# TensorE's sums of units 2 and 4 behind two u projections, and two step sizes and one scan input later on GpSimd

## The reference

```python
x = x + relu(sum over k of Xk @ Wk[k] + bk[k])       # graph layer, Xk = transition^k @ layernorm(x)
x = x + fc2(mamba(fc1(layernorm(x))))
# mamba: u, z = split(W_in h); u = silu(causal conv of 4 taps(u) + conv_b)
# dt, B, C = split(W_xproj u); delta = softplus(W_dt dt + b_dt); A = -exp(A_log)
h = exp(d_t[..., None] * A) * h + (d_t * u_t)[..., None] * B_t[:, None, :]   # scan over t
y_t = einsum('bds,bs->bd', h, C_t)
# y = (y + u * D) * silu(z), then W_out
```

## Time and profile before

| | us |
|---|---|
| median of 3 runs (3755.41 to 3759.54) | 3758.61 |
| the profiled execution's own time | 3757.91 |
| its span | 3756.1 |

### The profile page before, as it was taken

The page is one execution under the profiler, slowest core; times in us unless marked ns, Lnnn a source line. Parts: engine busy times, 40 slices in busy tenths (PEclk is TensorE's granted clock), DMA queues, the critical chain, the costliest instruction groups (busy, mean ns, idle before and its releaser), DMA issues.

```text
span 3756.1 us, 43683 instructions
## 1 busy us (share of the span) xinstructions
PE 3466.2 (92%) x11130; PEld 1957.4 (52%) x11130; DVE 3524.5 (94%) x2877; ACT 2954.1 (79%) x6578; POOL 3415.5 (91%) x1703
## 2 busy tenths in 40 slices
PE   6899999999999999999999999999999999999888
PEld 3555555555555555555555555555555555555434
DVE  0499999999999999999999999999999999999998
ACT  2588878888878888888788888788887888887774
POOL 0299999999999999999999999999999999999998
PEclk8899999999999999999999999999999999999999
DMA  3111101111100111110111110111110111110110
GB/s 111 53 56 58 58 10 52 55 58 58 58 23 38 55 58 58 58 39 22 58 55 58 58 56 8 55 55 58 58 58 9 53 55 58 58 54 12 42 51 9
DMA packets 50720, 183.68 MB, mean 49 GB/s; under 512 B 7356, under 2 KB 33220, under 8 KB 42086
## 3 DMA queue, kind: packets, MB, share of 16 engines
q1 hardware_dynamic: 48898, 174.17, 12.0%
q10 hardware_dynamic: 1636, 7.83, 0.5%
HBM read 164.15 MB, written 17.83 MB: 48 GB/s over the span
## 4 chain that ended last, share of the span: by engine, by line
POOL 54%; issue 31%; PE 7%; DVE 3%; ACT 3%; POOLq 1%; DMA 0%; SPq 0%; ACTq 0%; DVEq 0%
POOL st L425 40%; POOL st L416 7%; POOL delta L398 3%; POOL du_sb L406 3%; PE y_ps L771 2%; DVE st L953 1%; DVE st L965 1%; PE d_ps L808 1%; ACT dec L491 1%; POOL rstd L383 1%; POOLq L192 1%; PE g L924 1%; ACT L491 0%; PE dec L700 0%; DMA rows<-bk_dram 0%
## 5 line engine op out<-in xcount | busy, mean ns | idle before, releaser
L425 POOL TENSOR_TENSOR st<-st,bc 128x1024 f32<-128x1024 f32 x1024 | 2407.4, 2365 | 173.6 <-DVE st L965 172.8
L965 DVE TENSOR_TENSOR_SCAN st<-dec,st 128x1024 f32<-128x1024 f32 x1024 | 2313.0, 2274 | 12.1 <-POOL st L416 6.0
L771 PE MATMUL y_ps<-st,ident 128*128 128x512 f32 x4096 | 1947.4, 609 | 179.3 <-POOL st L425 177.6
L491 ACT ACTIVATE dec<-delta,decay 128x254 f32<-128x254 f32 x4096 | 1688.5, 462 | 286.4 <-DVE st L965 284.5
L771 PEld LDWEIGHTS y_ps<-st,ident 128*128 128x128 f32 x4096 | 748.1, 191 | 998.2 <-issue 628.0
L953 DVE TENSOR_TENSOR st<-du,bc 128x1024 f32<-128x1024 f32 x736 | 883.3, 1200 | 2.5 <-ACT du L477 2.2
L416 POOL TENSOR_TENSOR st<-du_sb,bc 128x1024 f32<-128x1024 f32 x288 | 681.5, 2367 | 0.1
L539 ACT ACTIVATE u<-d_ps,bconv,chan 128x256 f32<-128x256 f32 x256 | 130.0, 558 | 335.7 <-PE d_ps L808 335.7
L990 DVE SCALAR_TENSOR_TENSOR u<-d_ps,chan,u 128x250 f32<-128x250 f32 (+2 forms) x768 | 307.5, 468 | 58.7 <-ACT u L539 58.5
L808 PE MATMUL d_ps<-xnT,wxz 128*128 128x256 f32 x1024 | 257.0, 396 | 7.8 <-DVE u L990 7.1
L828 PE MATMUL d_ps<-xnT,wxz 128*128 128x256 f32 x1024 | 246.5, 384 | 14.6 <-ACT zs L552 14.2
(11 more groups left out here) (111 smaller groups left out, 2509.0 us busy)
## 6 DMA issues: line engine op xcount, KB each, us to landing
bc<-bc_dram SPq DMA_DIRECT2D x64, 2048.0 KB, 9.8
xg<-x_dram SPq DMA_DIRECT2D x32, 256.0 KB, 11.4
x_dram<-xg SPq DMA_DIRECT2D x32, 256.0 KB, 2.0
last_x<-x_dram SPq DMA_DIRECT2D x32, 256.0 KB, 2.6
out_dram<-last_x SPq DMA_DIRECT2D x32, 256.0 KB, 2.1
bc<-w_inT_dram ACTq DMA_DIRECT2D x1, 4096.0 KB, 13.9
adjt<-adjT_dram SPq DMA_DIRECT2D x32, 128.0 KB, 11.1
bc<-w_out_dram ACTq DMA_DIRECT2D x1, 2048.0 KB
```

The costliest lines, as they stand in the source:

```text
L425: nc.gpsimd.tensor_tensor(st[:, sl, :, :, :], st[:, sl, :, :, :], bc[:, p, 1, SU * q:SU * q + SU, None, :].to_broadcast([P, SU, 2, T]), AL ...
L491: a = nc.scalar.activation(dec[:, v % 2, s, j, :].rearrange("p (b t) -> p b t", b=PAIR)[:, :, 1:], delta[:, p, 2 * i + j, :].rearrange("p ...
L771: mm = nc.tensor.matmul(y_all, ident[:, :], st[:, sl, s, :, :].rearrange("p j t -> p (j t)"), start=False, stop=(q == Q - 1 and s == SU - ...
L965: nc.vector.tensor_tensor_scan(h, dec[:, v % 2, :, :, :].rearrange("p s j t -> p (s j t)"), h, 0.0, ALU.mult, ALU.add).then_inc(S["scanned ...
```

## The change

The sum of unit 2 moves from step 3 to step 4, where it stands behind the u projection and ahead of sum 3. The sum of unit 4 moves from step 5 to step 6, behind the u projection and ahead of sum 5. The step size of channel pair 2 moves from step 2 to step 10, that of pair 3 from step 6 to step 14, and the scan input of pair 2 from step 9 to step 11, each behind the product of its step.

```diff
-POOL_DELTAS = {0: 1, 2: 2, 6: 3}
-POOL_DUS = {2: 1, 9: 2, 17: 3}
+POOL_DELTAS = {0: 1, 10: 2, 14: 3}
+POOL_DUS = {2: 1, 11: 2, 17: 3}
@@ body of the TensorE list, in `if scan:`
                         if v % Q == 2:
                             state_sum(pe, k, p, v - 2)
-                        if v % Q != 1 and v > 0:
+                        if v in (4, 6):
+                            state_sum(pe, k, p, v - 2)
+                        if v % Q != 1 and v > 0 and v not in (3, 5):
                             state_sum(pe, k, p, v - 1)
```

## The result

The changed kernel takes 3736.4 us (median of 6 runs, 3729.5 to 3742.2) against 3757.1 (median of 6, 3755.4 to 3759.5) for the kernel before: ratio 0.9943, 95% interval 0.9933 to 0.9953. It is faster by some 21 us. I had forecast 3710 with a range of 3698 to 3728, so the gain is 21 us in place of the 48 that I worked out. Its runs also differ more among each other (13 us) than those before (4 us).

What follows compares the result with a forecast made beforehand. VectorE, 94% busy, was taken as the bound, GpSimd as a second. 28 bodies going from 111.93 to 110.4 us give 42.8, with the first and last bodies 48.4 us: 3710 us, range 3698 to 3728.

Steps and rivals of the forecast that it cites:

- The tap waits go: VectorE's convolution taps at steps 5 and 7: waits for ScalarE's u projection copy fall from 58.5 to 0 to 10 us.
- The gate, paced by product 6, becomes the limit: VectorE's gate at step 10 waits about 0.25 us for sum 7, behind GpSimd's product 6; a body takes 110.36 us.
- Body 1, body 30, body 31: Gains beside the 28 bodies: 2.7 us up to body 1's taps, 2.0 in body 30 less 0.3, 1.2 in body 31.
- Half clock behind the remaining gap: TensorE, behind about 2.0 us idle ahead of the first projection: costs some 1.6 us, 0.05 on the mean body.
- What I listed behind the projection: TensorE from step 4: projection, graph, sum 2, sum 3, graph, projection, sum 4, sum 5, all within 14.8 us.
- Rival 3: Half clock on TensorE's gapless stretch behind sum 6, 1.6 us each time on gate and scan 16: 3772 us; chance 5%.
- Rival 2: GpSimd's lateness felt at the second gate, step 18: 3739 us, or 3724 for half; chance 16% with the half.
- The rule weighed: Idle gaps between TensorE's bursts throttle it: the shorter first gap helps, the wait for product 6 could slow the gate.

Runs made afterwards that it cites:

- old-pool kernel: Changed kernel with sum 2 directly behind the projection of step 4, but GpSimd's step sizes and scan input where they were before the change: 3752.9 us, ratio 0.9987.
- inject kernel: Changed kernel with sum 2 directly behind the projection of step 4, and GpSimd's inject of unit 8 at step 6 behind product 6: 3698.6 us, ratio 0.9844.
- sums_only: Changed kernel with the new order of the sums, but GpSimd's step sizes and scan input where they were before: 3756.5 us, ratio 0.9997.
- pool_only: Kernel before the change, with only GpSimd's step sizes and scan input moved later as in the changed kernel: 3746.9 us, ratio 0.9973.
- sum2_first: Changed kernel with sum 2 directly behind the projection of step 4, ahead of the graph layer's first block: 3710.8 us, ratio 0.9878.
- block2_early: Changed kernel with the graph layer's second block at step 4 ahead of sums 2 and 3, instead of step 5 behind them: 3736.0 us, ratio 0.9938.
- filler kernel: Changed kernel with two matmuls of a zero stationary tile on TensorE in the gap ahead of the projection of step 4: 3712.1 us, ratio 0.9881.

## Why the prediction was wrong

The forecast had the right sign and the right account of an undisturbed body; one term, half clock behind the remaining gap, was mis-sized, and with it the path on which it falls. Step by step, by the two profiled executions:

- *The tap waits go.* Right: 58.5 to 6.1 us. The projection starts when the taps before it end.
- *The gate, paced by product 6, becomes the limit; an undisturbed body is 110.36 us.* Right: 110.37 measured. The gate waits 0.5 us, not 0.25, and VectorE was there that much earlier. The old-pool kernel and the inject kernel show the path from both sides.
- *Body 1, body 30, body 31 bring 2.7, 2.0 - 0.3 and 1.2 us.* Right: gate to gate they bring 2.2 (from the first scan to the gate of body 1), 2.0 and 1.2. The lead-in, ahead of everything that was changed, was 3.1 us shorter (first scan at 163.6 instead of 166.7), which is luck of the execution: up to the first scan `sums_only`, `pool_only` and `sum2_first` are the same program too, and there it starts at 166.4, 166.5 and 164.3.
- *Half clock behind the remaining gap costs TensorE 1.6 us, and the mean body 0.05 us.* Wrong, and this is the whole miss. I took length and price of the stretch from the rows before, where sum 2 came directly behind the gap. The change put the projection and a graph block there, and the stretch lasted 10.2 us, not 3.4: 5 us of TensorE, 3.4 of them on the body, or 1.2 us on the mean body instead of 0.05. That the order alone sets the length is not shown, see `sums_only` above. Ten bodies of 28: the mean is (3439.54 - 315.28) / 28 = 111.58 us from gate to gate, not 110.4. The 28 bodies bring 9.6 us where I had 42.8; the 33 us that are missing are ten bodies with 3.4 us too much. With the other terms, 9.6 + 3.1 + 2.2 + 2.0 + 1.2 is the 18.1 us by which the spans differ (3756.1 - 3738.0).
- *What I listed behind the projection.* The list was complete, but I named no user for the second graph block. It had 1.8 us to spare in undisturbed bodies, so 5 us of delay left 3.2.
- *The rivals.* Rival 3 had half clock on the stretch behind sum 6; in the changed kernel it stayed on the first stretch, which I had as harmless (0.7 us). Rival 2 did not occur: no idle piece of VectorE at steps 16 to 24.
- *The rule weighed.* The Trainium skill (TensorE: Matmul & The Clock Gate, "HAM oscillation — how this bites in real kernels") tells of waits of some 3 to 5 us between bursts that bring the clock down. The trace agrees, and with less: 2.0 us did in one body of three, 0.31 in none. I had drawn from it that a shorter gap helps, and it does in number (10 falls instead of some 18). I had not asked what it does in length.

The wider spread of the runs fits this: executions would differ in how many bodies are hit, at up to 3.4 us each. In `block2_early` the fastest run (3723.4 us) had a mean granted clock of 0.986, the others (3735.5 to 3741.2) 0.979 or 0.980. In the changed kernel the six clocks (0.979 to 0.982) are not in the order of the times, and only one execution of each kernel was profiled, so this is argued. The filler kernel, without such stretches, has a spread of 3.5 us.

## What to carry to other kernels

When an edit reorders TensorE behind a gap in which its clock may fall, price the fall anew: its length can change with the order behind the gap and from body to body, and so does who waits there. If a gap cannot be closed, try the order behind it and read the granted clock of every body; here sum 2 as the second piece of work kept all stretches at 3.4 us and off the critical path. Real work moved into a gap opens the same gap later, if a fixed event ends the stretch; look where that one stands. Two edits that each take away one of two nearly equal limits are to be judged together: alone they brought 0 and 10 us here, with the order of one sum put right 46.

## What was not expected of the hardware

TensorE can be busy without a break for some 10 us and stay at 1.2 GHz (1741 to 1751, granted clock 0.50). Behind a gap of the same length it was back in 3.4 us where a sum came second, and in the unchanged order too where the clock had fallen within 0.35 us of the restart (`sums_only`). Extra matmuls of a zero tile in a gap kept the clock up and were worth 24 us (9 us in the kernel before).
